# Cross attention of a four-layer kernel: context rows loaded three batches ahead, a Newton root split over two steps, and two groups of TensorE work moved in its order

## The reference

```python
def attention(q, k, v, mask):
    scores = jnp.einsum('bhqd,bhkd->bhqk', q, k) / jnp.sqrt(jnp.float32(HD))
    scores = scores * mask - 10000.0 * (1.0 - mask)
    probs = jax.nn.softmax(scores, axis=-1)
    return jnp.einsum('bhqk,bhkd->bhqd', probs, v)
ln_out = layernorm(hidden_states, ln1_s, ln1_b)
q, k, v = jnp.split(ln_out @ w_qkv + b_qkv, 3, axis=-1)
x = hidden_states + merge_heads(attention(..., ltor_mask)) @ w_ao + b_ao
ln_out = layernorm(x, ln2_s, ln2_b)
q = ln_out @ w_q + b_q
k, v = jnp.split(encoder_states @ w_kv + b_kv, 2, axis=-1)
x = x + merge_heads(attention(..., cross_mask)) @ w_co + b_co
```

## Time and profile before

| | us |
|---|---|
| median of 3 runs | 2642.47 (2639.51 to 2645.42) |
| profiled execution, its own time | 2640.79 |
| its span | 2639.1 |
| `layer2`, from the first window's values (L1936) to the last's | 1678.8 to 2059.9 |

### The profile page before, as it was taken

How to read it: one execution, slowest core, us unless ns; L and a number is a source line. 1 busy time by engine, 2 the same in 40 slices (tenths; PEclk the granted TensorE clock), 3 DMA queues, 4 the chain that set the end, 5 groups by cost and what they waited for, 6 DMA issues and landing times. The chain is left out here.

```text
span 2639.1 us, 53798 instructions
## 1 busy us (share of the span) xinstructions
PE 2293.1 (87%) x17161; PEld 1913.2 (72%) x17161; DVE 1933.2 (73%) x4994; ACT 1521.2 (58%) x4037; POOL 808.8 (31%) x978
## 2 busy tenths in 40 slices
PE   4999999977999999969788887588988696888886
PEld 4998989966989999969566665355555595677763
DVE  7666666676666666675899998777777665888866
ACT  2554545544555555556466666477766572667676
POOL 3011111120111111030444443466666303555530
PEclk9999999998999999989799999799999897999998
DMA  4100111010000100010000001000000000000000
GB/s 116 21 21 22 21 22 53 21 28 13 21 21 21 21 21 1 1 32 0 5 8 7 7 7 36 31 7 1 12 15 16 6 0 5 9 8 8 7 2 32
DMA packets 75321, 46.88 MB, mean 18 GB/s; under 512 B 31632, under 2 KB 74000, under 8 KB 75152
## 3 DMA queue, kind: packets, MB, share of 16 engines
q1 hardware_dynamic: 75152, 44.63, 6.6%
HBM read 41.46 MB, written 2.10 MB: 17 GB/s over the span
## 5 line engine op out<-in xcount | busy, mean ns | idle before, releaser
L1337 ACT ACTIVATE probs_t<-bank,zero 128x512 f32<-128x512 f32 x512 | 332.4, 685 | 110.5 <-PE bank L886 108.3
L2195 POOL TENSOR_TENSOR q_spread<-q_packed,part_of_head 128x512 fp32r<-128x512 f32 x256 | 262.7, 1058 | 377.0 <-DVE q_packed L1672 268.4
L1710 DVE TENSOR_REDUCE maxima<-bank 128x2 f32<-128x512 f32 x512 | 343.2, 679 | 36.0 <-PE bank L896 31.9
L1242 ACT ACTIVATE wide_probs_t<-bank 128x256 f32<-128x256 f32 x256 | 98.5, 385 | 311.6 <-PE bank L762 309.4
L2090 POOL TENSOR_TENSOR wide_columns<-wide_pair_columns,zero 128x8 f32<-128x8 f32 x16 | 3.3, 204 | 862.3 <-DVE x L1590 820.3
L886 PE MATMUL bank<-q_spread,k_packed 128*128 128x256 f32 x1024 | 249.8, 327 | 4.6 <-ACT probs_t L1337 2.5
L896 PE MATMUL bank<-k_packed,q_spread 128*128 128x256 f32 x1024 | 215.5, 295 | 35.1 <-DVE maxima L1710 20.1
L1247 ACT ACTIVATE wide_probs<-bank,wide_neg_max 128x129 f32<-128x129 f32 x512 | 184.1, 365 | 84.3 <-DVE wide_neg_max L1560 80.0
L1254 ACT ACTIVATE wide_heads_high<-bank,wide_columns 128x128 fp32r<-128x128 f32 x512 | 160.3, 365 | 96.0 <-PE bank L774 94.6
L1565 DVE RECIPROCAL wide_inverse<-wide_sums 128x2 f32<-128x2 f32 x256 | 42.4, 166 | 224.9 <-ACT wide_probs L1247 224.9
L886 PEld LDWEIGHTS bank<-q_spread,k_packed 128*128 128x128 f32 x1024 | 168.9, 194 | 46.7 <-ACT probs_t L1337 21.6
(11 more groups left out here) (274 smaller groups left out, 6920.8 us busy)
## 6 DMA issues: line engine op xcount, KB each, us to landing
cn<-in_ctx SPq DMA_DIRECT2D x48, 128.0 KB, 2.0
wide_pair_weights<-in_L_xattn_wq SPq DMA_DIRECT2D x16, 256.0 KB, 2.9
wide_pair_weights<-in_L_xattn_wk SPq DMA_DIRECT2D x16, 256.0 KB, 3.2
wide_pair_weights<-in_L_xattn_wv SPq DMA_DIRECT2D x16, 256.0 KB, 3.6
wide_pair_weights<-in_L_xattn_wo SPq DMA_DIRECT2D x16, 256.0 KB, 3.4
wide_ctx_rows<-in_ctx SPq DMA_DIRECT2D x4, 512.0 KB, 4.5
x<-in_x SPq DMA_DIRECT2D x4, 512.0 KB, 5.6
wide_pair_rows<-in_L_xattn_bv SPq DMA_DIRECT2D x16, 128.0 KB, 4.2
```

Source lines behind the costliest of these rows:

```text
L1337: act.activation(probs_t[j % 8][:, :], shifted_bank[j % 2][:, :], ACT.Exp, bias=zero[:, 0:1]).then_inc(s.exp_ready, 1)
L1710: dve.tensor_reduce(maxima[1 - u][:, j, :], head_scores[packed_scores(1 - u, j)][:, :].rearrange("p (a k) -> p a k", a=UNITS), X_AXIS, ALU ...
L2195: pool.tensor_tensor(q_spread[slot][:, first:first + SPREAD, :], q_packed[slot][:, pack:pack + 1, :].bitcast(F32).broadcast_to(wide), part ...
```

## The change

Four pieces of `layer2` and of the loads that serve it. On TensorE the transposes of the finished heads go from the end of step 0 to step 1, behind that step's transposes of the probabilities, and the q projection goes from ahead of the sums and the value projection of step 3 to behind them. On VectorE `roots` is cut in two: its first five instructions stay in step 1, the other six (two rounds of Newton) run in step 2 behind `qk`, and the normalization goes from step 2 to step 3, behind the maxima. On SyncE's queue the rows of a batch are issued one place earlier: ahead of the mask of the batch before it. Number and kind of the instructions stay as they are.

```diff
--- before.py
+++ after.py
@@ -1045,6 +1045,13 @@
                         for m in range(PACK):
                             last = pe.transpose(turn_bank[:, m * P:(m + 1) * P], probs[t][:, m * P:(m + 1) * P], ident[:, :])
                         last.then_inc(s.probs_turned, 1)
+                    if late and j == 1:
+                        pe.wait_ge(s.heads_taken, n - 2)
+                        if core:
+                            pe.wait_ge(s.v_ready, n + 1)
+                        for c in range(DC):
+                            last = pe.transpose(heads_bank[:, c * P:(c + 1) * P], heads_out[0][:, c * P:(c + 1) * P], ident[:, :])
+                        last.then_inc(s.heads_turned, 1)
                     if soon and j == 1:
                         layer, b = soon
                         keys_of = cn_t[1 - u] if layer else rows_t[1 - u]
@@ -1068,14 +1075,6 @@
                             last = pe.matmul(rows_bank, heads_t[0][:, c * P:(c + 1) * P], w_out2[:, layer, c, :],
                                              start=c == 0, stop=c == DC - 1)
                         last.then_inc(s.result, 1)
-                    if ahead and j == 3:
-                        layer = ahead[0]
-                        pe.wait_ge(s.in_ready, n + 3)
-                        after(pe, s.qk_ready, n + 2)
-                        for m in range(DC):
-                            for c in range(DC):
-                                pe.matmul(project2_bank[:, m * P:(m + 1) * P], w_qkv[:, layer, c, m * P:(m + 1) * P],
-                                          rows_t[u][:, c, :], start=c == 0, stop=c == DC - 1)
                     if past:
                         pe.wait_ge(s.probs_copied, g - 3)
                         if j == 0:
@@ -1085,13 +1084,6 @@
                             last = pe.matmul(sums2_bank[m * QUAD:(m + 1) * QUAD, j * P:(j + 1) * P], vn[1 - u][:, 0, PACK * j + m, :],
                                              probs_t[j][:, m * P:(m + 1) * P], start=True, stop=True)
                         last.then_inc(s.sums, 1)
-                    if late and j == 0:
-                        pe.wait_ge(s.heads_taken, n - 2)
-                        if core:
-                            pe.wait_ge(s.v_ready, n + 1)
-                        for c in range(DC):
-                            last = pe.transpose(heads_bank[:, c * P:(c + 1) * P], heads_out[0][:, c * P:(c + 1) * P], ident[:, :])
-                        last.then_inc(s.heads_turned, 1)
                     if soon and j == 3:
 
                         layer, b = soon
@@ -1101,6 +1093,14 @@
                             last = pe.matmul(rows_bank, keys_of[:, c, :], w_qkv[:, layer, c, 2 * D:3 * D],
                                              start=c == 0, stop=c == DC - 1)
                         last.then_inc(s.values, 1)
+                    if ahead and j == 3:
+                        layer = ahead[0]
+                        pe.wait_ge(s.in_ready, n + 3)
+                        after(pe, s.qk_ready, n + 2)
+                        for m in range(DC):
+                            for c in range(DC):
+                                pe.matmul(project2_bank[:, m * P:(m + 1) * P], w_qkv[:, layer, c, m * P:(m + 1) * P],
+                                          rows_t[u][:, c, :], start=c == 0, stop=c == DC - 1)
 
             over_sequence(pe, window)
 
@@ -1887,15 +1887,24 @@
                 dve.sem_inc(idle, 1)
                 chain.mark(dve.bn_aggr(stats.mean_var[:, k, :], stats.sums[:, k, :]))
 
-            def roots(m):
-
+            def roots(m, part):
+
+                rstd, shifted, work = stats.rstd[:, 0:SLOTS], stats.shifted[:, 0:SLOTS], stats.work[:, 0:SLOTS]
                 chain = Chain(dve, s.norm_chain, PAIR // SLOTS * m)
                 chain.steps = 2 * SLOTS
-                chain.join()
-                dve.sem_inc(idle, 1)
-                inverse_root(dve, chain, stats.rstd[:, 0:SLOTS], stats.mean_var[:, 0:SLOTS, 1], stats.shifted[:, 0:SLOTS],
-                             stats.work[:, 0:SLOTS])
-                dve.sem_inc(s.norm_chain, 1)
+                if not part:
+                    chain.join()
+                    dve.sem_inc(idle, 1)
+                    chain.link(dve.tensor_scalar(shifted, stats.mean_var[:, 0:SLOTS, 1], EPS, None, ALU.add))
+                    chain.link(dve.tensor_scalar(rstd.bitcast(I32), shifted.bitcast(I32), -0.5, 1597463007.0, ALU.mult, ALU.add))
+                else:
+                    chain.steps += 2 + 3
+                for _ in range(1 + part):
+                    chain.link(dve.scalar_tensor_tensor(work, rstd, -0.5, rstd, ALU.mult, ALU.mult))
+                    chain.link(dve.tensor_tensor(work, work, shifted, ALU.mult))
+                    chain.link(dve.scalar_tensor_tensor(rstd, work, 1.5, rstd, ALU.add, ALU.mult))
+                if part:
+                    dve.sem_inc(s.norm_chain, 1)
 
             def normalize(m, b, u):
 
@@ -1938,14 +1947,16 @@
                     if u and at(4) and j == 0:
                         measure(n + 4, at(4)[1], 1)
                     if u and coming and j == 1:
-                        roots(n + 3)
+                        roots(n + 3, 0)
                     if soon and j == 2:
                         layer = soon[0]
                         dve.wait_ge(s.projected, n + 2)
                         dve.tensor_tensor(qk[1 - u][:, :, :], project2_bank[:, :].rearrange("p (m q) -> p m q", m=2 * DC),
                                           b_qk2[:, layer, :, :].rearrange("p a c -> p (a c)").unsqueeze(2).broadcast_to([P, 2 * DC, P]),
                                           ALU.add).then_inc(s.qk_ready, 1)
-                    if coming and j == 2:
+                    if u and coming and j == 2:
+                        roots(n + 3, 1)
+                    if coming and j == 3:
                         normalize(n + 3, coming[1], 1 - u)
                     if soon and soon[0] and j == 3:
 
@@ -2378,20 +2389,28 @@
 
         def load_masked():
 
-            def load_mask(u, b):
+            def load_context_rows(u, b, first):
+                if not first:
+                    sp.wait_ge(n2.turned, b + (B - 1))
+                load_rows(n2.loaded[u], u, b)
+
+            def load_mask(u, b, first):
+                if not first:
+                    sp.wait_ge(n2.mask_added, STEPS * b + STEPS * (B - 1))
                 sp.dma_start(cross_mask[u][:, 0, :], t["mask_Bx1xSxS2_ff1"][ds(b, 1)].rearrange("b a q k -> q (b a k)"))\
                   .then_inc(n2.mask_loaded[u], 16)
 
+            for b in range(SLOTS):
+                load_context_rows(b, b, True)
+                load_mask(b, b, True)
+            load_context_rows(0, 2, False)
+            with sp.Fori(0, ROUNDS - 2) as i:
+                for u in range(SLOTS):
+                    load_context_rows(1 - u, SLOTS * i + u + 3, False)
+                    load_mask(u, SLOTS * i + u + 2, False)
+            load_context_rows(1, B - 1, False)
             for u in range(SLOTS):
-                load_rows(n2.loaded[u], u, u)
-                load_mask(u, u)
-            with sp.Fori(1, ROUNDS) as i:
-                for u in range(SLOTS):
-                    last = B + SLOTS * (i - 1) + u + 1
-                    sp.wait_ge(n2.turned, last)
-                    load_rows(n2.loaded[u], u, SLOTS * i + u)
-                    sp.wait_ge(n2.mask_added, STEPS * last)
-                    load_mask(u, SLOTS * i + u)
+                load_mask(u, B - SLOTS + u, False)
 
         attend(0, pk.in_ready)
 
```

## The result

The changed kernel takes 2654.3 us (median of 5 runs, 2652.6 to 2658.3) against 2642.5 before (also the median of five runs): ratio 1.0042, 95% interval 1.0026 to 1.0057. It is slower by 11.9 us between the medians. The forecast was slower by 23.3, to 2664, in a range of 2631 to 2679.

The account below looks back on a forecast made before the run. No engine is full; chains that change engine bound the windows. Terms -11.6, -1.4, -1.1, +5.7, +16.2 and -3.5 gave +4.3 us, the clock +19: +23.3 on the profiled 2640.8, so 2664 us, range 2631 to 2679.

Parts of the forecast that it names:

- Context rows, normalization and window 29: Cross attention: earlier rows save 11.6 us in even windows, the normalization's move costs 5.7, window 29 loses a 1.4 wait.
- Heads' transposes: Even self windows: TensorE no longer idles for vn but waits for ScalarE's copy; -1.1 us over seven windows.
- Window 1: No late batch, so values don't wait; TensorE stays busy and the clock should hold: -3.5 us.
- Root split and q projection: Thirteen odd windows: GpSimd blocks part two, delaying addition to x, value and q projections; +1.2 us each, +16.2 with mask.
- The clock: Odd windows: 2.8 us of TensorE idle lowers its clock in ten of thirteen, 1.9 us each: +19.
- A: Rival: windows stretched but the clock holds, +4.3 us alone, 2645 us, no measurable change; chance 0.13.
- B: Rival: faster, part two free of GpSimd, normalization and mask free, clock steady; 2624 us; chance 0.19 with its mixture.
- C: Rival: the clock falls and stays low twice as long in nearly all odd windows; 2679 us; chance 0.12.
- D: Rival: the early load takes no effect, transposes still wait for the context rows; 2675 us; chance 0.04.
- The limit given for B: B decides when an odd window loses under 1.2 us in all, clock included.
- the mask's term: Cross windows: moved normalization makes it and the mask's second form meet GpSimd, delaying VectorE; +5.7 us in even ones.
- signs named ahead: Odd windows: addition to x 6.7 us behind the root's start, TensorE waits about 2.8, windows take 14 us or more.

Follow-up runs that it names:

- e3: The kernel before with only the earlier issue of the context rows; 2623.4 us, ratio 0.9936.
- e7: The changed kernel with the normalization back in step 2, behind qk or part two of the root; 2647.2 us, ratio 1.0022.
- e9: The changed kernel with the root whole in step 1, normalization in step 2, and odd windows' addition to x right behind the root; 2612.7 us, ratio 0.9896.
- e11: e9 with the transposes of the finished heads back at the end of step 0; 2616.8 us, ratio 0.9894.
- e5: The changed kernel with the q projection computed twice, once more ahead of the value projection; 2650.3 us, ratio 1.0038.
- e1: The changed kernel with the q projection alone put back ahead of the sums and value projection; 2633.7 us, ratio 0.9973.
- e2: The changed kernel with the root whole again in step 1; 2624.7 us, ratio 0.9936.
- e4: The changed kernel with the addition to x, in odd windows with a root, moved between qk and part two; 2627.1 us, ratio 0.9941.
- e6: The changed kernel with the six links of part two replaced by one-input reductions (coarser result); 2627.9 us, ratio 0.9946.
- e10: e9 with the q projection back ahead of the sums and the value projection; 2642.1 us, ratio 0.9996.

## Why the prediction was right, and where its sizes were off

*Context rows, normalization and window 29.* Forecast -11.6 + 5.7 = -5.9 in the even cross windows, measured 84.0 - 90.1 = -6.1; window 29 -1.4, measured -1.4. That the sum hits so well is luck: apart, e3 gives the rows -10.7 in these windows, 0.9 less than forecast, and e7 the normalization's place 4.4, 1.3 less, and the two misses cancel.

*Heads' transposes.* -1.1 forecast in the even self windows, -0.4 measured: the wait for `vn` (9.4) went, and the one for `probs_t` (13.5, 0.8 before) came in its place, 0.50 where the other had been 0.72. Windows 10 and 12 gain that 0.2 each; 4, 6 and 8 gain nothing, and what binds them is not shown. e9 against e11 shows where the new place pays: 1.1 us in the even self and 3.2 in the even cross windows.

*Window 1.* 15.65 became 11.74, -3.9 for -3.5.

*Root split and q projection.* The mechanism is as forecast, and the chain came as it was worked out: the first two links wait for GpSimd, the addition comes 10.14 behind the window's first mask product (10.2 forecast), TensorE waits 2.93 (2.8). From the value projection to the next mask product are 3.20 us, not 3.37, and it starts 0.05, not 0.15, behind the addition. So a self window costs +0.92 (13.81 against 12.89), not +1.2. The four without a fall (9, 11, 15, 27) cost 0.92, 0.63, 1.06 and 1.05; in the cross loop, where the changed kernel has none, e5 gives 14.18, +1.29. For thirteen that is 13.8 instead of 16.2. It takes the split and the order together: against before, the odd windows cost 10.6 with the split but not the order (e1, one fall), 2.1 with the order but not the split (e2, two falls) and 27.5 with both; the other pieces are in all three. e4, with the addition out of the split's reach, is at 12.95 in the self loop, and e6, whose links don't wait for GpSimd, at 12.84.

*The clock.* Ten falls at 1.9, +19, were forecast. The profile has nine, and with e5 as measure they cost 13.7, 1.5 each on average. The term that was mis-sized most is this price of a fall. It was taken as the mean of window 1 and window 26. But in window 1 the clock stayed low twice as long as in eight of the nine (window 25 is the other, with 2.4 us), and of its 2.8 one microsecond was longer waiting (2.48 against 1.48 ahead of the q projection) and no price of the clock. How often it would fall was an estimate with no rule behind it, and that nine came for ten is in part luck: within the changed kernel a wait of 2.93 did not lower it and one of 2.46 did.

In sum the layer costs 14.9 where 23.3 was forecast: 5.3 of the gap are the clock, 2.4 the odd windows' stretch, the rest the small terms. The remaining 3 us down to 11.9 between the medians are not settled. Only one execution has a trace, and it was the slowest of its five; and in ten of the eleven comparisons with the kernel before the medians give 1 to 6 us less than the layer, so part of it may lie in the single trace of before.

Of the rivals, A (no fall) would be 2645; its stretched odd windows are nearly those of e5, which has a single fall. B needed the port free and the clock steady, and e6 has the first but not all of the second. C (low twice as long in nearly all) came in one window of thirteen, 25. D is out: no transposes wait for the context's load any more. The limit given for B was a little off: without the mask's term the other pieces give back 17.6 us, 1.35 for each of the thirteen windows and not 1.2. Of the signs named ahead, the addition to x came 6.6 behind the root's start (6.7 forecast), but four windows stayed under 14 us, at 13.2 to 13.8, since the clock held there.

## What to carry to other kernels

A long chain of small instructions is best left where GpSimd is idle: cut in two, its second half stood in front of the one instruction that TensorE waited for, and under GpSimd's long ones. Before moving work behind a wait, compare which of the two waits ends last in the new order: the q projection behind the value projection cost 16.9 us in the odd windows with the addition to x late (changed kernel against e1), and gained 21.0 with it early (e9 against e10). And idle time of TensorE has a second price in its clock: where a wait grows from 1.5 to 2.9 us, count 1.2 to 1.65 us more for each window in which the clock falls, and more where it stays low for longer.

## What the runs showed of the hardware

A VectorE link of 0.16 us with two tensors in SBUF took 1.00 us under a GpSimd instruction, and a reduction with a single input took under 0.2 at the same place (e6). A single input was no safeguard for other instructions: the normalization took 0.98 to 1.14 where it started under GpSimd's addition in its new place, and 0.40 in its old one.

The granted clock fell behind TensorE waits of 2.46 to 3.12 us in nine of the thirteen odd windows of the changed kernel. The length of the wait alone did not decide it: window 9 held behind 2.93. Behind 1.8 the clock fell in two windows of e2 and held in two, and it fell behind 1.26 in one window of e1, where six other waits of that length left it alone. It held behind all thirteen waits of 1.23 to 1.48 in the odd windows of e3, and behind those of e9, at most 0.9. With matrix work put into the wait (e5, at most 1.9 left) it fell once.
